# Attention of a gated cross-attention block: the value products of two steps issued together at the end of the odd step

## The chip, the cores and the metric

The kernel runs on one core of a Trainium2 chip. The metric is device time in microseconds (us) of one execution. The core has five instruction streams that run side by side and meet only at semaphores: PE (TensorE, matmuls, with its weight loads shown as PEld), DVE (VectorE), ACT (ScalarE), POOL (GpSimd) and SP (SyncE, which only issues DMAs here). Each stream is executed in the order in which it is written.

## The reference, cut to what matters

```python
# x (4,512,256), ctx (4,1024,256); 16 heads of 64; everything float32
lat = layer_norm(_layernorm(x), lat_g, lat_b);  ctx = layer_norm(ctx, ctx_g, ctx_b)
q = heads(lat @ Wq);  k, v = split(ctx @ Wkv);  k = rope(heads(k), cos, sin);  v = heads(v)
attn = softmax(clip(q @ k.T * 64**-0.5, -11, 11))
x = x + tanh(g_xattn) * (merge(attn @ v) @ Wo + bo)
# then a mixture of 4 experts, 2 per token (router, gelu MLP 256-1024-256), on layer_norm(x):
x = x + tanh(g_ffn) * moe(_layernorm(x))
```

## The kernel before

The attention is cut into 4 batches `b`, 4 units `u` of four heads, and 8 steps `s` per unit. A unit has two pairs of heads; steps 0 to 3 belong to the first pair and 4 to 7 to the second, and `c = s % 4` is the place within the pair. In the text a step is also given by `i = 8*u + s` (0 to 31 within a batch). A step takes 256 positions of the context, in two halves. For them it computes the scores of two heads against 512 queries (`score`, line 1909), exponentiates them (`exps`, ACT, line 989), clamps the result between the exponentials of -11 and 11 (`clamp`, DVE, line 1231, which writes `prob[:, s % 2]` in place), adds the probabilities to the running denominators (`sums`, DVE, line 1237; none at c = 0) and multiplies them with the values (`values`, PE, line 1924, 16 matmuls on 32-column strips of the array that accumulate in PSUM).

Beside that each step makes keys and values for the next unit: `kv_make` (PE, line 1890) multiplies, `kv_evac` (ACT, line 935) copies out, `rot_cos` (DVE, line 1218) and `rotate` (POOL, line 752, two operations, L757 and L761) apply the rotary embedding, and in the following step `k_turn` (PE, line 1901, L1906 in the profile) transposes the rotated keys into the bank `tr`. It first waits for `rot`, that is for POOL's second operation. `k_split` (ACT, line 929) and `k_low` (DVE, line 1183, L1186) then empty `tr`. All float32 products are made of three products of rounded parts (`three`, line 1861; lines 1863 to 1865).

The order on PE is written by hand in `step` (line 2044): the two score halves; `k_turn` of the previous step and `kv_make` (in steps i = 19 to 28 of a batch that has a successor, and in i = 9 and 10, `kv_make` comes first); at c = 0 `denominators` (L1946); at s = 2 and 3 the projection of the unit before (`project`); at c = 1 `q_make`; then `values` of the previous step; then, in steps i = 18 to 27 of batches 0 to 2, one transpose for the next batch's context or input into `tr` (`ctx_turn` L1870, `lat_turn` L1877), and in steps i = 8 and 9 one for the router (`x_turn` L1980). These transposes wait for `k_ready`, which `k_low` of the same step raises, since they write the bank that it reads. In the last unit of the last batch (`is_direct`) there are no keys to make and `direct` (L1961) sums the denominators on PE behind the values.

The scores of a step wait until the exponentials of the step before have read the same PSUM bank. `values` waits for the two clamps of its own step, and at c = 0 also for `normalise` (DVE, L1268) of the pair before, which reads the same output bank `pv`. The order on DVE within a step is: `q_low` (c = 2) or `normalise` (c = 1); clamp; clamp; `rot_cos`; `k_low`; `ctx_low` where the next batch is prepared; the two `sums`; `residual`; `reciprocals` (c = 0) or `o_low` (c = 1); statistics and normalisation of rows. POOL has, besides `rotate`, small scale computations for the next batch (`ctx_scale`, `lat_scale`, lines 717 to 742) and in the last batch the scatters of rows.

Of the kernel before, what the change touches and what calls it, by code (L numbers as in the profile page):

```python
# [33 lines left out]
def flamingo_kernel(nc, x, ctx_in, g_xattn, g_ffn, cos, sin, lat_g, lat_b, ctx_g, ctx_b, w_q, w_kv, w_o, b_o,  # L34
# [9 lines left out]
    UNITS = INNER // (4 * DH)  # L44
# [4 lines left out]
    STEPS = 2 * CH  # L49
# [15 lines left out]
    with ExitStack() as stack:  # L65
# [291 lines left out]
        def step_no(b, u, s):  # L357
            return b * BS + (u * STEPS + s)

        def tile_no(b, t):  # L360
            return b * ST + t

        def kv_no(b, u, t):
            return b * BS + (u * ST + t)

        def pair_no(b, p):
            return b * PAIRS + p
# [10 lines left out]
        def wait(eng, semaphore, count):  # L378

            if count > 0:  # L380
                eng.wait_ge(semaphore, count)
# [69 lines left out]
        def is_direct(b, u):  # L451

            return b == B - 1 and u == UNITS - 1

        def out_bank(b, p):

            return tr if b == B - 1 and p == PAIRS - 1 else pv
# [5 lines left out]
        def den_bank(b, p):  # L463

            return kv if b == B - 1 and p == PAIRS - 2 else mi
# [32 lines left out]
        def is_first(b, u):  # L498
            return b == 0 and u == 0
# [5 lines left out]
        def next_unit(b, u):  # L505
            return (b, u + 1) if u + 1 < UNITS else (b + 1, 0)

        def next_pair(b, p):
            return (b, p + 1) if p + 1 < PAIRS else (b + 1, 0)
# [1348 lines left out]
        def _(pe):  # L1858
# [31 lines left out]
            def kv_make(b, u, t):  # L1890
                pe.wait_ge(c_ready, tile_no(b, t) + 1)
                if b == 0 and t == 0:
                    pe.wait_ge(wkv_ready, u + 1)
                wait(pe, rot1, t - 1 if is_first(b, u) else kv_no(b, u, t))
                for k in range(KT):
                    last = three(kv_bank(b, u, t)[:].rearrange("p (w n) -> p w n", w=2), lambda l: ctx_t[:, l, k, t * P:(t + 1) * P],
                                 lambda l: wkv[:, l, k, :].rearrange("p (w n) -> p w n", w=2)[:, :, u * UW:(u + 1) * UW],
                                 k == 0, k == KT - 1)
                last.then_inc(kv_ready, 1)
# [9 lines left out]
            def score(b, u, s, i):  # L1909
                c, j, p = s % CH, s // CH, u * 2 + s // CH  # L1910
                t = 2 * c + i
                pe.wait_ge(k_ready, kv_no(b, u, t) + 1)
                if c == 0 and i == 0:
                    pe.wait_ge(q_ready, pair_no(b, p) + 1)

                wait(pe, exp_done[i], step_no(b, u, s))
                for lk, lq in ((0, 0), (0, 1), (1, 0)):
                    for h in range(2):
                        rows_h = slice(h * DH, (h + 1) * DH)
                        last = mm(sc[i][:, h * N:(h + 1) * N], kst[rows_h, u % 2, j, lk, t * P:(t + 1) * P],  # L1920
                                  q_sp[rows_h, p % 2, lq, :], start=lk + lq == 0, stop=lk == 1)
                last.then_inc(sc_ready[i], 1)

            def values(b, u, s):
                c, j, p = s % CH, s // CH, u * 2 + s // CH
                if c == 0 and out_bank(b, p) is tr:
                    pe.wait_ge(k_ready, B * BS)
                elif c == 0:

                    wait(pe, o_norm, pair_no(b, p))  # L1930
                for i in range(2):
                    pe.wait_ge(clamped[i], step_no(b, u, s) + 1)
                    for g in range(4):
                        half, h = g // 2, g % 2
                        at = (2 * j + h) * DH + half * 32
                        last = mm(out_bank(b, p)[g * 32:(g + 1) * 32, :], val[:, u % 2, 2 * c + i, at:at + 32],  # L1936
                                  prob[:, s % 2, i, h * N:(h + 1) * N], start=c == 0 and i == 0, stop=c == CH - 1 and i == 1)
                last.then_inc(pv_done, 1)
# [11 lines left out]
            def direct(b, u, s):  # L1950

                c, p = s % CH, u * 2 + s // CH
                if c == 0:
                    pe.wait_ge(den_turned, pair_no(b, p))
                    if p == PAIRS - 2:
                        pe.wait_ge(rot1, B * BS)
                for i in range(2):
                    for g in range(4):
                        half, h = g // 2, g % 2
                        at = h * N + half * QH  # L1960
                        last = mm(den_bank(b, p)[g * 32:(g + 1) * 32, 0:QH], ones[:, 0:32], prob[:, s % 2, i, at:at + QH],  # L1961
                                  start=c == 0 and i == 0, stop=c == CH - 1 and i == 1)
                if c == CH - 1:
                    last.then_inc(den_ready, 1)
# [79 lines left out]
            def step(b, u, s, last):  # L2044
                i = u * STEPS + s
                p, c = u * 2 + s // CH, s % CH
                make = not (last and u == UNITS - 1)
                nb, nu = next_unit(b, u)
                score(b, u, s, 0)
                score(b, u, s, 1)  # L2050
                asked = i - X_TURN in (1, 2)
                turned = asked or not last and 0 <= i - TURN - 1 < ST + 2
                if make and turned:
                    kv_make(nb, nu, s)
                if i == X_TURN + 3:
                    pe.wait_ge(f_lout, 2 * b + 3)
                if last and i == R_RANK + 3:
                    pe.wait_ge(r_read, 1)
                if s == 0 or make:

                    if asked:
                        router(b, i - X_TURN - 1, tr, 0, UW // E)
                    elif turned and i - TURN - 1 < ST:
                        pe.wait_ge(c_affd, tile_no(b + 1, i - TURN - 1) + 1)
                    elif turned:
                        pe.wait_ge(l_affd, 2 * (b + 1) + i - L_TURN)
                    k_turn(*((nb, nu, s - 1) if s else (b, u, ST - 1)))
                if make and not turned:
                    kv_make(nb, nu, s)
                if c == 0 and not (is_first(b, u) and s == 0):  # L2070

                    pe.wait_ge(q_ready, pair_no(b, p) + 1)
                    wait(pe, wo_out, (b * UNITS + u) * 2 - (2 if s == 0 else 0))
                    if not (is_direct(b, u) and s == CH):
                        denominators(*((b, p - 1) if p else (b - 1, PAIRS - 1)))
                if s in (2, 3) and not is_first(b, u):

                    pe.wait_ge(q_ready, pair_no(b, p + 1) + 1)
                    wait(pe, wo_out, (b * UNITS + u) * 2 + s - 4)
                    project(*((b, u - 1) if u else (b - 1, UNITS - 1)), s - 2)  # L2080
                if c == 1 and not (last and p == PAIRS - 1):

                    wait(pe, den_turned, pair_no(b, p))
                    q_make(*next_pair(b, p))
                if not (is_first(b, u) and s == 0):
                    values(*((b, u, s - 1) if s else (b, u - 1, STEPS - 1) if u else (b - 1, UNITS - 1, STEPS - 1)))
                if is_direct(b, u) and s:
                    direct(b, u, s - 1)
                if not last and TURN <= i < L_TURN + 2:

                    pe.wait_ge(k_ready, kv_no(nb, nu, s - 1) + 1 if s else kv_no(b, u, ST - 1) + 1)
                    if i < L_TURN:
                        ctx_turn(b + 1, i - TURN, tr)
                    else:
                        lat_turn(b + 1, i - L_TURN, tr)
                if i - X_TURN in (0, 1):

                    pe.wait_ge(k_ready, kv_no(nb, nu, s - 1) + 1 if s else kv_no(b, u, ST - 1) + 1)
                    pe.wait_ge(f_lout, 2 * b + i - X_TURN + 1)
                    pe.wait_ge(f_norm, b * NT + 2 * (i - X_TURN) + 2)  # L2100
                    x_turn(i - X_TURN, tr)
                if last and i == R_RANK + 1:
                    pe.wait_ge(k_ready, kv_no(nb, nu, s - 1) + 1)
                    count_slots()
                if is_direct(b, u) and s == SLOTS_AT:
                    pe.wait_ge(den_turned, B * PAIRS - 1)
                    slots_turn(0)
# [122 lines left out]
```

## Time and profile before

| | |
|---|---|
| median of 3 runs | 1106.79 us (1106.78 to 1106.92) |
| the profiled execution | 1109.79 us, span of its instructions 1108.1 us |
| mean granted clock of TensorE | 0.995 |
| busy over the span | PE 96%, DVE 85%, PEld 64%, ACT 59%, POOL 48% |
| the chain that ended last | PE 78%, DVE 14%, issue 3%, ACT 2% |
| attention steps | from 37 us to 849 us of the span |

A timeline row gives the start in us from the span's start, the time until its last instruction ends, the engine, the line, the operation, output and inputs with their shapes, and how many instructions are merged. In brackets stands the idle time of the engine before it and what ended it. A window row gives its bounds and length, the busy time (and number of instructions) of PE, PEld, DVE, ACT and POOL, the granted clock, the share of the DMA engines and their GB/s. The ends of matmuls are modelled, so the start of the next instruction tells more than the end of the last.

### The profile page before, as it was taken

Reading aid. Unit: us, or ns where it says so; the run is one execution under the profiler, and the core shown is the slowest. Engines: PE = TensorE matmul, PEld = TensorE weight load, DVE = VectorE, ACT = ScalarE, POOL = GpSimd, SP = SyncE. Lnnn points to the kernel's source line nnn. Section 1 sums busy time; section 2 is a strip of 40 time slices with the busy share of each in tenths; the row PEclk is TensorE's granted clock in tenths of the full one; section 3 lists DMA queues with packets and bytes.
Section 4 is the critical chain, followed back from the end, with each engine's and each line's share of the span. In section 5 each row is a group of like instructions: output and inputs, shape, how many; then the busy total and the mean of one; then the engine's idle time right before and its main releaser. Section 6 shows DMA issues by size and latency. Waiting matters only on the chain.

```text
span 1108.1 us, 22494 instructions
## 1 busy us (share of the span) xinstructions
PE 1069.2 (96%) x7965; PEld 712.2 (64%) x7965; DVE 946.6 (85%) x1765; ACT 655.8 (59%) x1269; POOL 532.3 (48%) x551
## 2 busy tenths in 40 slices
PE   5999999999999999999999999999999999999996
PEld 3556555655555555656555655665546998899995
DVE  7898999898989989898999898879988756876676
ACT  5655556664645765555566655544568565667663
POOL 7433375332437634342565353424761655655561
PEclk9999999999999999999999999999999999999998
DMA  7000010000000000001010000610165333555335
GB/s 200 25 10 11 20 39 11 20 11 11 10 20 23 27 11 11 13 8 30 1 44 15 11 11 10 192 54 20 50 213 181 106 116 130 178 194 189 116 115 181
DMA packets 60054, 73.10 MB, mean 66 GB/s; under 512 B 11420, under 2 KB 53032, under 8 KB 59945
## 3 DMA queue, kind: packets, MB, share of 16 engines
q1 hardware_dynamic: 56376, 62.87, 18.5%
q0 software_dynamic: 3264, 8.53, 2.0%
q8 instruction: 66, 1.08, 0.4%
q14 instruction: 44, 0.35, 0.1%
q10 hardware_dynamic: 304, 0.27, 0.1%
HBM read 54.84 MB, written 17.33 MB: 65 GB/s over the span
## 4 chain that ended last, share of the span: by engine, by line
PE 78%; DVE 14%; issue 3%; ACT 2%; DMA 1%; POOL 1%; another core or an unknown queue 0%; SPq 0%; DVEq 0%; POOLq 0%
PE pv L1936 16%; PE sc L1920 15%; PE kv L1863 6%; PE kv L1865 5%; PE kv L1864 5%; PE sc L1863 4%; PE sc L1865 4%; PE sc L1864 4%; PE tr L1906 3%; DVE acc L1249 3%; PE mi L1863 3%; PE mi L1864 2%; PE mi L1865 2%; PE mi L1946 2%; DVE prob L1234 2%
## 5 line engine op out<-in xcount | busy, mean ns | idle before, releaser
L997 ACT ACTIVATE prob<-sc 128x1024 f32<-128x1024 f32 x256 | 249.3, 1029 | 194.9 <-PE sc L1920 187.0
L757 POOL TENSOR_TENSOR rot_s<-k_raw,sinb 128x256 f32<-128x256 f32 x128 | 110.4, 862 | 380.7 <-ACT k_raw L940 380.6
L1936 PE MATMUL pv<-prob,val 128*32 128x512 f32 x1984 | 237.8, 597 | 1.1 <-DVE recip L1268 0.6
L1234 DVE TENSOR_SCALAR prob<-prob 128x1024 f32<-128x1024 f32 x256 | 183.2, 729 | 40.5 <-ACT prob L997 38.1
L1920 PE MATMUL sc<-q_hid,w2all 64*128 64x512 f32 x1536 | 213.3, 409 | 0.0
L1920 PEld LDWEIGHTS sc<-q_hid,w2all 64*128 64x128 f32 x1536 | 134.8, 185 | 100.2 <-issue 55.2
L1249 DVE TENSOR_TENSOR acc<-acc,prob 128x1024 f32<-128x1024 f32 x120 | 177.6, 1501 | 0.0
L761 POOL TENSOR_TENSOR rot_c<-rot_c,rot_s 128x256 f32<-128x256 f32 x128 | 109.6, 856 | 39.4 <-DVE rot_c L1222 24.9
L1936 PEld LDWEIGHTS pv<-prob,val 128*32 128x32 f32 x1984 | 54.8, 109 | 106.5 <-issue 86.9
L1863 PE MATMUL kv<-w2all,acts 128*128 128x512 f32 x248 | 109.9, 443 | 2.0 <-DVE acts L1180 2.0
L1865 PE MATMUL kv<-w2all,acts 128*128 128x512 f32 x248 | 98.6, 398 | 0.0
L1864 PE MATMUL kv<-w2all,acts 128*128 128x512 f32 x248 | 98.0, 395 | 0.0
L1863 PE MATMUL sc<-w2all,q_hid 128*128 x296 | 87.2, 295 | 7.3 <-DVE q_hid L1717 6.5
L1246 DVE TENSOR_TENSOR acc<-prob 128x1024 f32<-128x1024 f32 x60 | 84.8, 1452 | 0.0
L1864 PE MATMUL sc<-w2all,q_hid 128*128 x296 | 83.8, 283 | 0.0
L1865 PE MATMUL sc<-w2all,q_hid 128*128 x296 | 83.6, 282 | 0.0
L940 ACT ACTIVATE k_raw<-kv 128x256 f32<-128x256 f32 x124 | 48.6, 392 | 50.6 <-PE kv L1865 48.5
L1222 DVE TENSOR_TENSOR rot_c<-kv,cosb 128x256 f32<-128x256 f32 x124 | 52.1, 420 | 28.9 <-ACT val L941 23.0
L1717 DVE SCALAR_TENSOR_TENSOR q_hid<-sc,rot_c,q_hid 128x256 fp32r<-128x256 f32 x78 | 37.6, 482 | 36.5 <-ACT q_hid L1115 30.8
L1110 ACT ACTIVATE sc<-sc,c_aff 128x256 f32<-128x256 f32 x78 | 34.9, 448 | 54.2 <-PE sc L1865 50.2
L838 POOL TENSOR_TENSOR acts<-prob,acts 128x512 fp32r<-128x512 f32 x34 | 45.0, 1322 | 40.8 <-ACT acts L1030 39.6
L1863 PEld LDWEIGHTS sc<-w2all,q_hid 128*128 128x128 f32 x296 | 56.5, 191 | 10.4 <-issue 10.2
(346 smaller groups left out, 2409.9 us busy)
## 6 DMA issues: line engine op xcount, KB each, us to landing
prob<-in_L_ffn_w SPq DMA_DIRECT2D x17, 1024.0 KB, 5.2
slots_x<-lat_r SPq DMA_DIRECT2D x1, 5016.0 KB, 18.2
rows<-slots_x SPq DMA_DIRECT2D x19, 264.0 KB, 5.2
rows<-in_ctx SPq DMA_DIRECT2D x32, 128.0 KB, 2.2
w_raw<-in_L_xattn_Wq SPq DMA_DIRECT2D x16, 256.0 KB, 2.7
w_raw<-in_L_xattn_Wo SPq DMA_DIRECT2D x64, 64.0 KB
acc<-in_L_ffn_w SPq DMA_DIRECT2D x16, 256.0 KB, 4.1
acc<-in_L_ffn_w SPq DMA_DIRECT2D x5, 512.0 KB
```

What stands on the lines that cost most here:

```text
L757: g.tensor_tensor(rot_s[:].rearrange("p (h a c) -> p h a c", h=4, a=2), kh[:, :, ::-1, :], sinb[:, t].unsqueeze(1).to_broadcast([P, 4, 2, ...
L761: g.tensor_tensor(k_rot[:], rot_c[:], rot_s[:], ALU.add).then_inc(rot, 1)
L997: a.activation(prob[:, s % 2, i, :], sc[i][:], ACT.Exp, scale=DH ** -0.5).then_inc(exp_done[i], 1)
L1222: v.tensor_tensor(rot_c[:].rearrange("p (h c) -> p h c", h=8), kv_bank(b, u, t)[:, 0:UW].rearrange("p (h c) -> p h c", h=8), cosb[:, t].un ...
L1234: v.tensor_scalar(prob[:, s % 2, i, :], prob[:, s % 2, i, :], EXP_LOW, EXP_HIGH, ALU.max, ALU.min).then_inc(clamped[i], 1)
L1246: v.tensor_tensor(acc[:, i, :], prob[:, 0, i, :], prob[:, 1, i, :], ALU.add).then_inc(summed[i], 1)
L1249: v.tensor_tensor(acc[:, i, :], acc[:, i, :], prob[:, s % 2, i, :], ALU.add).then_inc(summed[i], 1)
L1863: mm(dst, lhs(0), rhs(0), start=start, stop=False, **kw)
L1864: mm(dst, lhs(0), rhs(1), start=False, stop=False, **kw)
L1865: return mm(dst, lhs(1), rhs(0), start=False, stop=stop, **kw)
L1920: last = mm(sc[i][:, h * N:(h + 1) * N], kst[rows_h, u % 2, j, lk, t * P:(t + 1) * P], q_sp[rows_h, p % 2, lq, :], start=lk + lq == 0, sto ...
L1936: last = mm(out_bank(b, p)[g * 32:(g + 1) * 32, :], val[:, u % 2, 2 * c + i, at:at + 32], prob[:, s % 2, i, h * N:(h + 1) * N], start=c == ...
```

## The change

In every unit but the last unit of the last batch, an even step issues no value products; an odd step issues those of the step before and its own, one behind the other, at the place where one such block stood. The last unit of the last batch keeps its order, but its first step has no block of the unit before any more, since the odd step 7 has issued it.

```diff
@@ PE, step(b, u, s, last)
                     wait(pe, den_turned, pair_no(b, p))
                     q_make(*next_pair(b, p))
-                if not (is_first(b, u) and s == 0):
-                    values(*((b, u, s - 1) if s else (b, u - 1, STEPS - 1) if u else (b - 1, UNITS - 1, STEPS - 1)))
                 if is_direct(b, u) and s:
+                    values(b, u, s - 1)
                     direct(b, u, s - 1)
+                elif s % 2 and not is_direct(b, u):
+                    values(b, u, s - 1)
+                    values(b, u, s)
                 if not last and TURN <= i < L_TURN + 2:
```

## Rows read from the trace of the kernel before

**Rows 1.** Busy time of each engine and granted clock (PEclk), attention steps.
```profile
37.00:849.00 812.00, 804.55 (x5888) 459.93 (x5892) 735.40 (x1250) 472.56 (x865) 365.74 (x377) 1.00 0.11 35
```
**Rows 2.** Timeline of PE, steps i = 14 and 15 of batch 2.
```profile
532.83 1.67 PE L1920 MATMUL sc<-q_hid,w2all 64*128 64x512 f32 x12
534.43 0.44 PE L1906 MATMUL tr<-ident,rot_c 128*128 128x128 f32 x2
...
535.87 0.40 PE L1865 MATMUL kv<-w2all,acts 128*128 128x512 f32 x1
536.20 1.92 PE L1936 MATMUL pv<-prob,val 128*32 128x512 f32 x16
538.05 1.65 PE L1920 MATMUL sc<-q_hid,w2all 64*128 64x512 f32 x12
...
543.26 1.66 PE L1920 MATMUL sc<-q_hid,w2all 64*128 64x512 f32 x12
```
**Rows 3.** Timelines of ACT, DVE and POOL, the same two steps.
```profile
533.85 1.94 ACT L997 ACTIVATE prob<-sc 128x1024 f32<-128x1024 f32 x2 [2.17 <-PE sc L1920]
...
537.40 0.41 DVE L1186 TENSOR_TENSOR w2all<-tr,w2all 128x256 fp32r<-128x256 f32 x1
537.74 2.85 DVE L1249 TENSOR_TENSOR acc<-acc,prob 128x1024 f32<-128x1024 f32 x2
...
540.51 1.28 DVE L1234 TENSOR_SCALAR prob<-prob 128x1024 f32<-128x1024 f32 x2
...
537.64 0.73 POOL L761 TENSOR_TENSOR rot_c<-rot_c,rot_s 128x256 f32<-128x256 f32 x1
```
**Rows 4.** Timeline of PE, step i = 28 of batch 3: values, direct, score.
```profile
830.57 1.92 PE L1936 MATMUL pv<-prob,val 128*32 128x512 f32 x16
832.31 1.05 PE L1961 MATMUL kv<-prob,ones 128*32 128x256 f32 x16
833.29 1.65 PE L1920 MATMUL sc<-q_hid,w2all 64*128 64x512 f32 x12
```
**Rows 5.** Timelines of PE and DVE, step i = 20 of batch 2.
```profile
574.12 1.07 PE L1946 MATMUL mi<-acc,ones 128*32 128x256 f32 x16
575.01 1.90 PE L1936 MATMUL pv<-prob,val 128*32 128x512 f32 x16
576.84 0.44 PE L1870 MATMUL tr<-ident,rows 128*128 128x128 f32 x2
577.21 0.97 PE L1920 MATMUL sc<-q_hid,w2all 64*128 64x512 f32 x6
...
575.27 0.41 DVE L1186 TENSOR_TENSOR w2all<-tr,w2all 128x256 fp32r<-128x256 f32 x1
```
**Rows 6.** Timelines of PE and DVE, step i = 22 of batch 2.
```profile
589.59 0.44 PE L1870 MATMUL tr<-ident,rows 128*128 128x128 f32 x2
...
589.12 0.41 DVE L1186 TENSOR_TENSOR w2all<-tr,w2all 128x256 fp32r<-128x256 f32 x1
```
**Rows 7.** Timelines of PE and DVE, step i = 8 of batch 2.
```profile
497.39 0.66 PE L1980 MATMUL tr<-ident,more 128*128 128x128 f32 x4
...
496.03 0.41 DVE L1186 TENSOR_TENSOR w2all<-tr,w2all 128x256 fp32r<-128x256 f32 x1
```
**Rows 8.** Timelines of POOL and PE, steps i = 16 and 17 of batch 2.
```profile
543.54 1.18 POOL L736 TENSOR_TENSOR l_rs<-l_mv,eps 128x4 f32<-128x4 f32 x1
...
550.34 0.73 POOL L761 TENSOR_TENSOR rot_c<-rot_c,rot_s 128x256 f32<-128x256 f32 x1
...
551.13 0.44 PE L1906 MATMUL tr<-ident,rot_c 128*128 128x128 f32 x2
```
**Rows 9.** Timeline of POOL, step i = 28 of batch 2 (begins at 624.17).
```profile
629.51 1.13 POOL L761 TENSOR_TENSOR rot_c<-rot_c,rot_s 128x256 f32<-128x256 f32 x1
```
**Rows 10.** Timelines of DVE and PE, batch 3, steps i = 15 and 25.
```profile
752.25 1.72 DVE L1234 TENSOR_SCALAR prob<-prob 128x1024 f32<-128x1024 f32 x2
...
814.39 1.92 PE L1936 MATMUL pv<-prob,val 128*32 128x512 f32 x16 [0.52 <-issue]
```

## The prediction

> **What bounds the kernel now.** I read the busy times over the attention steps first, then the timeline of PE through two plain steps, then the other engines in the same two steps. In the attention PE is busy 804.6 of 812.0 us at the full clock; DVE follows with 735.4, ACT has 472.6 and POOL 365.7 [rows 1]. The reader should see that PE hardly ever waits: each instruction of step 14 starts as the one before it drains [rows 2]. So a step costs what PE issues in it, and the other engines matter only where one of them makes PE wait. How near they are is in the third view. Keys made on PE in step 14 end at 535.87 + 0.40; ACT copies them, and POOL's second rotation ends at 537.64 + 0.73 = 538.37, which is 5.54 after the step's first score at 532.83 [rows 2, 3]. The transpose that needs them comes 1.60 into the next step, at 5.22 + 1.60 = 6.82. The slack of this chain is 1.3 us, and it exists because a block of values, 1.85 us, stands between the keys and the next step. That block is what the change takes out of even steps.
>
> **What a block costs and what joining saves.** From the first values matmul to the next score it is 538.05 - 536.20 = 1.85 [rows 2]; to a block that works on the same column strips it is 832.31 - 830.57 = 1.74 [rows 4]. I price the join of two value blocks at 1.74 + 1.85, so it saves 0.11. The entry is no saving: keys to values starts 0.33 after the last key matmul, and I take keys to score as the same, as both change the shape in the array. At c = 0 the denominators stand between: denominators to values takes 0.89 [rows 5], the same kind of block to a score 833.29 - 832.31 = 0.98 [rows 4], so 0.89 + 1.83 + 1.85 before and 0.98 + 1.74 + 1.85 after, which is 4.57 both times. So a pair of an even and an odd step gains 0.11 if c is 2 and 3, nothing if c is 0 and 1, where no wait is new. At best, if the shape change on both sides of a removed block (about 0.10 and 0.12) were all saved, it would be 0.22 in each of 60 pairs, 13 us; at worst joining saves nothing.
>
> The trace's 1.74 against 1.85 is a small gain from keeping the column strips. The Trainium skill (TensorE: Matmul & The Clock Gate, Part 3, The mechanism) says that weight loads overlap matmuls in flight only when the row group differs; all value matmuls use the whole height, so by it the join would drain like any other border and save nothing. The trace speaks against that, as 1.74 is less than 1.85.
>
> **Where PE will wait (the rotation).** Without the block step 14 is 536.20 - 532.83 = 3.37 long, and its successor wants the transposed keys at 3.37 + 1.60 = 4.97. POOL's add ends at 5.54 as before, since it hangs on ACT and on this step's keys, not on the values; PE resumes 0.06 behind it (550.34 + 0.73 = 551.07, then 551.13 [rows 8]). So PE waits 0.63 there. The pair takes 3.37 + 5.21 + 1.74 + 0.63 = 10.95 against 543.26 - 532.83 = 10.43: 0.52 more. This holds for pairs (6,7), (14,15) and (30,31) of a batch. The clamps of step 15 don't decide it, though closely: DVE's sums end at 540.59 and the two clamps at 541.79, 8.96 after the start [rows 3], and the second values block begins at 5.60 + 0.20 + 1.56 + 1.74 = 9.10. In pair (28,29) `kv_make` is first, the step would be 3.39 + 0.98 = 4.37, and POOL ends at 629.51 + 1.13 = 630.64, 6.47 after 624.17 [rows 9]: a wait of 6.53 - 5.96 = 0.57. In pair (16,17) POOL first has the scale chain of the next batch: from its start at 543.54 to the end of the add at 551.07 are 7.53 us [rows 8]. After the change it starts some 0.65 before step 16, when step 15's rotation is done, so the transpose goes at 6.94, not at 4.35 + 1.60: 1.00 of wait, of which 551.13 - 549.33 - 1.60 = 0.20 is there already (549.33 is the first score of step 17): 0.80 more. Pairs (0,1), (4,5) and (12,13) have the denominators, 4.35 + 1.60 = 5.95 against 5.60, and the project blocks of 1.4 us cover (2,3) and (10,11).
>
> **Where PE will wait (the bank `tr`).** The transposes for the next batch wait for `k_low`, which the values covered. In step 22 the values are no cover even now: `k_low` ends at 589.53 and the transpose starts at 589.59 [rows 6], 5.38 after the step's start at 584.21. Without the block PE is there at 3.40. `k_low` can't be done much before 4.84, since its chain goes through the exponentials, two copies and the clamps; in step 20 it ends at 575.27 + 0.41 = 575.68, 4.96 after 570.72 [rows 5]. With a transpose at 4.90 and 0.37 from it to the score [rows 5], steps 20, 22 and 24 become 5.27 to 5.30 long. They were 6.49, 5.75 and 6.48, and each gives 1.74 to its odd neighbour. Step 23 waits 0.6 for `k_low` today and no longer will. Per pair: (20,21) +0.55, (22,23) +0.64, (24,25) +0.55. Steps 18 and 26 have a project block and come out even (0 and -0.04). Step 8: `k_low` ends at 496.44, 5.12 after 491.32, the transpose at 497.39 leads to the score at 497.97 [rows 7]; with `k_low` at 4.98 the step is 5.62 instead of 6.65, and the pair gains 1.74 - 1.03 = 0.71 in length.
>
> **What queues behind the new waits.** Behind a waiting `k_turn` or transpose stand on PE the rest of the step and the next scores, behind which ACT's exponentials and then DVE's clamps stand. As odd steps grow by 1.74, DVE has caught up by the next even step, and no wait is passed on. No DMA, and no order on another queue, changes.
>
> **The sum.** Batches 1 and 2 each: 3 x 0.52 + 0.57 + 0.80 + 0.71 + 0.55 + 0.64 + 0.55 - 0.26 = 5.1. Batch 0: the same, 1.74 because the block of step 1 now stands in step 1, 0.63 for pair (2,3), which has no project block yet, and about 0.5 more at step 8: 8.0. Batch 3 prepares no batch but routes rows on DVE. 0.52 + 0.71 for pairs (6,7) and (8,9), -0.3 for those without a wait; in (14,15) the clamps of step 15 run at 752.25 to 753.97 [rows 10], 9.31 to 11.03 after step 14's start at 742.94, and the values of step 15 wait for them, +1.6, of which pair (16,17) gives 0.5 back; (20,21) waits 0.9 for POOL. That is 2.9, a sum of small walks, good to 3 us. The block that step 24 loses is no gain: values of step 24 stand at 814.39 after an idle time of PE [rows 10], held by DVE's chain to `normalise`, and whether PE gets there 1.85 earlier doesn't matter; this term lies between -1.85 and 0, and I take 0. The expert stage is not touched. Total 8.0 + 10.2 + 2.9 = 21.1 us. On the profiled execution, 1109.79 us (its span is 1108.1), that is 1130.9; it stands 3.00 above the median of the runs, so the forecast is 1106.79 + 21.1 = 1127.9, say 1128 us.
>
> **The rivals.** *The waits are larger.* The values of the odd step wait for its own clamps, for which the margin is 0.14 at the first half in pair (14,15). If DVE is 0.5 late in about half of the 60 pairs, 15 us come on top: 1143. For it speaks DVE's 91% in these steps [rows 1]; against it, that odd steps become longer and that the second half of a block has 0.85 more. If joining saves nothing, 0.11 x 60 = 6.6 come on top: 1134. Chance of over 1137: 0.14.
>
> *Faster, by the changes of shape.* If a removed border saves 0.22 in each of the 60 pairs, this is worth 13 us, and if copies and rotation are quicker when PE leaves them more time between bursts, so that the waits don't open, the time is 1094. It decides from the point where the key chain ends within 4.97 instead of 5.54. Against it: the chain's length is the same in nearly all plain steps, and every link of it is an engine's own duration. With the waits it is 1128 - 13 + 3 = 1118, still slower. Chance of a gain: 0.08.
>
> *No change.* The waits open, but what DVE and POOL were behind is made good in the longer odd steps, by about as much. Today's waits that could vanish are small: PE is idle 7.4 us of the attention in all [rows 1], against 21 of new ones. Near 1107, chance 0.05.
>
> **How the numbers follow.** The forecast's own case (1116 to 1137) has 0.73. A measurement of this kernel tells 0.2%, about 2.2 us, from no change. Faster 0.08, same 0.05, slower 0.87. The range takes the borders' ends (-10 and +6.6), and about a third of the waits either way: 1116 to 1138.
>
> **What would show it.** In the profile after: no values block in even steps, blocks of 32 matmuls some 3.55 us long in odd ones; idle time of PE or its weight loads before L1906 with POOL's L761 as releaser, 0.6 in steps 7, 15 and 31 of a batch and about 1.0 in step 17; idle time before L1870 and L1980 with DVE's L1186 as releaser, 1.4 in step 22; pair (14,15) 10.95 long, pair (4,5) unchanged at about 12.6. The forecast is wrong if POOL's add ends earlier after the score than 5.54, if the join costs or saves more than 0.11, or if the values of odd steps wait for the clamps (L1234) outside the last batch.

## The result and the profile after

The changed kernel takes 1133.22 us (median of 4 runs, 1132.55 to 1136.86) against 1106.86 (1106.78 to 1107.45) for the kernel before in the same session: a ratio of 1.025, 95% interval 1.0238 to 1.0262. It is slower by 26.4 us; 21 were forecast, as 1128 in 1116 to 1138. Its profiled execution took 1132.68 us, with a span of 1130.9.

First the busy times over the attention, which now ends at 875 and not at 849. The row has the same columns as [rows 1] and answers to it.

```profile
37.00:875.00 838.00, 801.61 (x5886) 463.09 (x5890) 739.86 (x1250) 472.05 (x864) 366.96 (x378) 1.00 0.11 34
```

PE was without work for 812.0 - 804.6 = 7.4 us and is now for 838.0 - 801.6 = 36.4. Its busy time even fell by 2.9. So the matmuls are not dearer: PE waits 29 us more. What it waits for is in the view of waits (engine and line that wait, engine and line that end it: us in total, times, longest), of the kernel after:

```profile
PEld tr L1906 <- POOL rot_c L761: 31.9, 37, 2.7
PE tr L1906 <- POOL rot_c L761: 17.2, 24, 2.5
PEld tr L1870 <- DVE w2all L1186: 16.0, 12, 2.2
PE tr L1870 <- DVE w2all L1186: 11.8, 12, 1.9
PEld pv L1936 <- DVE prob L1234: 11.4, 22, 2.3
```

The same rows of the kernel before:

```profile
PEld tr L1906 <- POOL rot_c L761: 13.6, 19, 2.4
PE tr L1906 <- POOL rot_c L761: 5.7, 6, 2.2
PEld tr L1870 <- DVE w2all L1186: 7.2, 6, 1.4
PE tr L1870 <- DVE w2all L1186: 1.6, 3, 0.5
PEld pv L1936 <- DVE prob L1234: 9.0, 28, 0.4
```

PE's own idle time before the key transposes grew by 11.5 us and before the next batch's transposes by 10.2, which is 21.7 of the 29. The rest is spread over the router's transposes (L1980), the input's (L1877) and, in batch 3, the values. Steps 14 to 17 of batch 2 on PE and POOL, which answer to [rows 2, 8], show how one such wait looks:

```profile
551.99 1.65 PE L1920 MATMUL sc<-q_hid,w2all 64*128 64x512 f32 x12
...
555.33 1.65 PE L1920 MATMUL sc<-q_hid,w2all 64*128 64x512 f32 x12
...
557.56 0.44 PE L1906 MATMUL tr<-ident,rot_c 128*128 128x128 f32 x2 [0.58 <-POOL rot_c L761]
...
559.33 3.64 PE L1936 MATMUL pv<-prob,val 128*32 128x512 f32 x32
562.90 1.67 PE L1920 MATMUL sc<-q_hid,w2all 64*128 64x512 f32 x12
...
570.17 0.44 PE L1906 MATMUL tr<-ident,rot_c 128*128 128x128 f32 x2 [1.26 <-POOL rot_c L761]
...
556.78 0.72 POOL L761 TENSOR_TENSOR rot_c<-rot_c,rot_s 128x256 f32<-128x256 f32 x1
...
561.89 0.73 POOL L761 TENSOR_TENSOR rot_c<-rot_c,rot_s 128x256 f32<-128x256 f32 x1 [0.96 <-DVE rot_c L1222]
562.58 1.18 POOL L736 TENSOR_TENSOR l_rs<-l_mv,eps 128x4 f32<-128x4 f32 x1
...
569.39 0.73 POOL L761 TENSOR_TENSOR rot_c<-rot_c,rot_s 128x256 f32<-128x256 f32 x1
```

Step 14 is 555.33 - 551.99 = 3.34 long, without a block of values. POOL's add ends at 557.50, 5.51 after the step's first score (5.54 was expected), and the transpose goes 0.06 later. The joined values take 562.90 - 559.33 = 3.57, where two single blocks took 3.70.

From the first scores of even steps comes the length of each pair of steps. This table is worked out from the timelines of PE; it has the change against the kernel before, in us, for batch 2 (for the kernels of the experiments too, which are told below):

```
pair      before  forecast  after     e1      e2     e3     e4     f2     f3     f4     g1
(0,1)     12.64      0      -0.01   +0.06   +0.01  +0.06   0.00  -0.02  +0.08  -0.01  +1.71
(2,3)     13.27    -0.11    -0.14   -0.10   -0.16  -0.11  -0.14  -0.14  -0.10   0.00  -0.14
(4,5)     12.64      0       0.00   +0.08    0.00  +0.08   0.00  +0.01  +0.08  +0.01  -1.71
(6,7)     10.43    +0.52    +0.49   -0.11   -1.22  -1.82  +0.48  +0.48  -1.82  -0.01  +0.40
(8,9)     14.72    +0.71    +0.69   +0.70   +2.31  +2.93  +0.69  +0.70  +1.72  +0.01  +2.32
(10,11)   14.15    -0.11    -0.13   -0.08   -0.12  -0.08  -0.13  -0.12  -0.08  -0.01  -0.12
(12,13)   12.64      0      +0.01   +0.08    0.00  +0.08  +0.01   0.00  +0.08  +0.01  -1.71
(14,15)   10.43    +0.52    +0.48   +0.40   +0.48  +0.40  +0.48  +0.48  -0.11  -0.01  -0.02
(16,17)   12.85    +0.80    +1.12   -0.13   -0.59  -1.83  +1.11  -0.21  -1.89  -0.21  +0.85
(18,19)   14.61      0      -0.46   +0.65*  +0.58  +1.43  -0.46  -0.46  +0.95  -0.30  -0.01
(20,21)   13.49    +0.55    +1.45   +1.40*   0.00   0.00  +1.47  +0.51   0.00   0.00   0.00
(22,23)   11.95    +0.64    +1.13   +2.64*  +0.02  +0.01  +0.65  +1.14  -0.57  -0.58   0.00
(24,25)   13.48    +0.55    +0.52   +0.51   +0.01  +0.01  +0.50  +0.51  +0.02  +0.01  +0.01
(26,27)   14.53    -0.04    +0.43   +0.42   +1.71  +1.71  -0.06  +0.44  +1.70   0.00   0.00
(28,29)   12.69    +0.57    +0.54   +0.07   +0.51  +0.07  +0.51  +0.54  +0.07  -0.01  -0.01
(30,31)   10.42    +0.52    +0.78   +0.72   +0.77  +0.72  +0.78  +0.50  -0.10   0.00   0.00
sum                 5.1      6.9     7.3     4.3    3.7    5.9    4.4    0.0   -1.1   +1.6
* batch 0 has -0.14, +0.52 and +1.13; why batch 2 differs is told with the first experiment
```

Where a kernel issues a block one pair earlier or later, two entries shift by 1.7 in opposite directions; there only sums over neighbours count. Batches 0, 1 and 3 of the kernel after have 9.6, 8.4 and 1.0, with 0.26 ahead of step 0; its attention ends 26.15 us later. The span grew by 22.8 only, because the profiled execution of before had a pause of 3.42 us in the expert stage that the profile after lacks, and stood 3.0 above its median (the columns of the row below are those of [rows 3]). Otherwise the expert stage is the same.

```profile
938.28 0.45 ACT L1110 ACTIVATE sc<-sc,c_aff 128x256 f32<-128x256 f32 x1 [3.42 <-remote]
```

### The profile page after: what moved, and what is told of

Same layout as the page of the kernel before. It is cut to its first block, busy times and chain, and to the rows that moved or that the text cites. A ratio compares the mean times of both kernels' runs of the same rounds, so it can differ in the third digit from the quotient of the medians.

```text
span 1130.9 us, 22494 instructions
## 1 busy us (share of the span) xinstructions
PE 1066.8 (94%) x7965; PEld 716.1 (63%) x7965; DVE 950.6 (84%) x1765; ACT 655.6 (58%) x1269; POOL 532.7 (47%) x551
## 4 chain that ended last, share of the span: by engine, by line
PE 70%; DVE 14%; issue 5%; ACT 4%; POOL 4%; DMA 1%; SPq 0%; DVEq 0%; POOLq 0%
PE pv L1936 16%; PE sc L1920 11%; PE kv L1863 5%; PE sc L1863 4%; PE kv L1865 4%; PE kv L1864 4%; PE sc L1864 4%; PE sc L1865 4%; DVE acc L1249 4%; PE tr L1906 3%; PE mi L1863 2%; PE mi L1865 2%; PE mi L1864 2%; ACT prob L997 2%; DVE prob L1234 2%
## 5 line engine op out<-in xcount | busy, mean ns | idle before, releaser
L757 POOL TENSOR_TENSOR rot_s<-k_raw,sinb 128x256 f32<-128x256 f32 x128 | 114.0, 890 | 386.5 <-ACT k_raw L940 386.4
L1234 DVE TENSOR_SCALAR prob<-prob 128x1024 f32<-128x1024 f32 x256 | 194.5, 773 | 55.2 <-ACT prob L997 53.5
L1936 PE MATMUL pv<-prob,val 128*32 128x512 f32 x1984 | 226.9, 595 | 4.1 <-DVE recip L1268 2.5
L1249 DVE TENSOR_TENSOR acc<-acc,prob 128x1024 f32<-128x1024 f32 x120 | 175.2, 1481 | 0.0
L1936 PEld LDWEIGHTS pv<-prob,val 128*32 128x32 f32 x1984 | 57.5, 109 | 134.4 <-issue 117.2
L1906 PE MATMUL tr<-ident,rot_c 128*128 128x128 f32 x256 | 54.2, 294 | 17.3 <-POOL rot_c L761 17.2
L1906 PEld LDWEIGHTS tr<-ident,rot_c 128*128 128x128 f32 x256 | 29.2, 144 | 54.1 <-POOL rot_c L761 31.9
```

Of the source, the lines that this page charges most:

```text
L757: g.tensor_tensor(rot_s[:].rearrange("p (h a c) -> p h a c", h=4, a=2), kh[:, :, ::-1, :], sinb[:, t].unsqueeze(1).to_broadcast([P, 4, 2, ...
L1234: v.tensor_scalar(prob[:, s % 2, i, :], prob[:, s % 2, i, :], EXP_LOW, EXP_HIGH, ALU.max, ALU.min).then_inc(clamped[i], 1)
L1249: v.tensor_tensor(acc[:, i, :], acc[:, i, :], prob[:, s % 2, i, :], ALU.add).then_inc(summed[i], 1)
L1906: last = nc.tensor.transpose(tr[:, j * P:(j + 1) * P], k_rot[:, j * P:(j + 1) * P], ident[:])
```

## The experiments

My theory after the first look was the prediction's: without its block, an even step comes to a transpose before the keys or the bank are ready. Two places were larger than forecast, (20,21) and (22,23), and there I blamed the order on DVE and ACT. The rival was that DVE, at 91% busy, is a second limit right beneath, so that no mended order on PE would win the waits back. The first four experiments ran on a chip on which the kernel before had 1110.31 us, the others on chips where it had 1106.07, 1109.68 and 1105.85. So times are compared by their ratios to the kernel before on the same chip; the kernel after has 1.025.

### Keys made first in every odd step

```diff
                 turned = asked or not last and 0 <= i - TURN - 1 < ST + 2
-                if make and turned:
+                early = turned or s % 2
+                if make and early:
                     kv_make(nb, nu, s)
...
-                if make and not turned:
+                if make and not early:
                     kv_make(nb, nu, s)
```

> The changed kernel, but in every odd step kv_make stands ahead of k_turn. Theory (PE waits because the block that covered the chain of keys is gone): the 0.6 us waits for POOL's add in steps 3, 7, 15 and 31, the 0.55 in 29 and the 1.2 in 17 go, 12.5 us in all, 1133.2 to about 1121. Rival (the odd step's values wait for DVE's clamps, and DVE sets the pace): nothing to gain, 1131 to 1134.

Measured: 1130.23 us, ratio 1.0172 (1.0133 to 1.0211). Some 8 us of the loss are gone by the ratios (6 by the pairs of the profiles), where 12.5 were expected: 1121 would have been a ratio of 1.013. The waits for POOL went as expected; steps 14 and 15 on PE, and DVE's clamps:

```profile
551.13 0.50 PE L1863 MATMUL kv<-w2all,acts 128*128 128x512 f32 x1
...
552.62 0.38 PE L1906 MATMUL tr<-ident,rot_c 128*128 128x128 f32 x2
552.93 1.92 PE L1936 MATMUL pv<-prob,val 128*32 128x512 f32 x16
555.16 1.92 PE L1936 MATMUL pv<-prob,val 128*32 128x512 f32 x16 [0.30 <-DVE prob L1234]
...
553.87 1.83 DVE L1234 TENSOR_SCALAR prob<-prob 128x1024 f32<-128x1024 f32 x2
```

The transpose stands behind the keys and waits for nothing, and 0.5 us later the values of step 15 wait for their own clamps. Pair (14,15) goes from +0.48 to +0.40, not to -0.11: one wait taken away uncovers another of nearly the same size. In (16,17), (28,29) and, in batches 1 to 3, (6,7) nothing takes the wait's place, and in (20,21) of batches 0 and 1 DVE's lag is gone (+0.52). The uncovered wait speaks for the rival.

Batch 2 shows how little slack DVE has. In step 18 it waited for rows of the next batch that a DMA brought:

```profile
571.75 0.43 DVE L1160 BATCH_NORM_STATS2 c_bn<-rows 128x6 f32<-128x256 f32 x1 [0.21 <-DMA rows<-in_ctx]
```

Against batch 1, where all ran alike until then, this instruction starts 0.28 later, `k_low` of the same step 0.77 later and that of the next step 1.18 later. PE waits for it in steps 18 and 20, and the pairs (18,19) and (20,21) cost 0.8 and 0.9 more than in batch 1, at the full clock. The excess of (22,23) is another thing, a stretch of TensorE at 1.2 GHz (last section).

### Single blocks kept ahead of the transposes

Odd steps 7 (all batches) and 17, 19, 21, 23, 25 (batches 0 to 2) issue only the block of the step before. The edit is shown against the kernel before; the call of `values` there is gone.

```diff
+            issued = [-1]
+            def joins(b, i):
+                return not (i == 7 or b < B - 1 and i in (17, 19, 21, 23, 25))
...
+                upto = step_no(b, u, s) - 1
+                if s % 2 and not is_direct(b, u) and joins(b, i):
+                    upto += 1
+                while issued[0] < upto:
+                    issued[0] += 1
+                    nb_, ni_ = divmod(issued[0], BS)
+                    values(nb_, ni_ // STEPS, ni_ % STEPS)
```

> The changed kernel, but the odd steps 7 (all batches) and 17, 19, 21, 23, 25 (batches that have a successor) issue only the values of the step before, so that the even steps with a transpose into tr behind them keep their block. Theory: pairs (8,9) and (18,19) to (26,27) return to their old lengths, -2.9 and -3.1 x 3, and the clock drop seen behind the 1.9 us wait in batch 1 goes: 1133.2 to about 1121. Rival (DVE sets the pace): less than 4 us back.

Measured: 1129.29 us, 1.017 (1.0139 to 1.0201), where 1.013 was expected. Steps 20 to 25 are as before the change, all 3.1 us of them won back in batch 2, so those waits are the missing blocks' doing. The stretch at 1.2 GHz in batch 1 is gone too, as expected. But (6,7) and (8,9) together are +1.09 after +1.18, although step 8 has its block again. Step 8 is 7.25 us long, not 6.65: its key transpose now waits 0.53 for POOL, behind the 0.59 in step 7.

### Both

> Both edits in one: keys first in odd steps, and blocks kept ahead of the transposes. Theory: the two kinds of wait are separate, so the gains add: 1133.2 - 12.5 - 12.3 = 1108.4, within 3 us of the kernel before. Rival (one underlying limit, DVE's load): the sum is clearly less than the parts, 1115 or more.

Measured: 1124.91 us, 1.0125 (1.0098 to 1.0151). It was expected within 3 us of before, and it is 14 above: the case of 1115 or more. The two edits don't add up. PE's waits for POOL at the key transposes fell from 17.2 to 7.4 us, and pairs (6,7) and (8,9) still cost -1.82 + 2.93 = 1.11. That is one wait for POOL in step 8:

```profile
501.97 0.44 PE L1906 MATMUL tr<-ident,rot_c 128*128 128x128 f32 x2 [1.14 <-POOL rot_c L761]
...
500.28 1.63 POOL L761 TENSOR_TENSOR rot_c<-rot_c,rot_s 128x256 f32<-128x256 f32 x1
```

POOL has the router's statistics ahead of this rotation (two operations, 1.19 and 2.24 us), and the add itself takes 1.63, where 0.73 is its usual time. So moving `kv_make` forward on PE can't help there.

### ACT's queries first

ACT rounds the next queries before it scales the next batch's rows, so that the exponentials behind them start earlier in steps 22 and 26.

```diff
+                if c == 1 and not (last and p == PAIRS - 1):
+                    q_round(*next_pair(b, p))
                 if not last and 0 <= i - TURN < ST:
...
-                if c == 1 and not (last and p == PAIRS - 1):
-                    q_round(*next_pair(b, p))
```

> The changed kernel, but on ACT q_round stands ahead of ctx_affine and lat_affine at c = 1. Theory (steps 22 and 26 gave nothing back because the exponentials stand behind the copy of the queries on ACT, at 1.97 instead of 1.49 after the score): these steps shrink by 0.48 each, 1133.2 to about 1130.3. Rival (k_low is late there because DVE lags): no change, 1133.

Measured: 1133.08 us, 1.0194 (1.0167 to 1.0221). The pairs moved just as expected, (22,23) from 1.13 to 0.65 and (26,27) from +0.43 to -0.06. These six moves are worth 2.9 us. The times are no measure of that: by the ratios the kernel is 6 us below the kernel after, and the profiled execution stood 2.6 above its median, with 3.06 more in (12,13) of batch 3 than the kernel after, where TensorE ran at 1.2 GHz for a stretch. So the cause at these two steps is shown by the pairs and not by the time.

### The kernel after once more, and each with light sums

To see what DVE does beneath, `sums` at c = 2 and 3 got 64 of 1024 columns, in the kernel after, in the kernel of both edits and in the kernel before. The denominators are incomplete; all waits stay.

```diff
-                    v.tensor_tensor(acc[:, i, :], acc[:, i, :], prob[:, s % 2, i, :], ALU.add).then_inc(summed[i], 1)
+                    v.tensor_tensor(acc[:, i, 0:64], acc[:, i, 0:64], prob[:, s % 2, i, 0:64], ALU.add).then_inc(summed[i], 1)
```

> The changed kernel itself, beside the three below on the same chip, since the chip of the first four edits ran the kernel before at 1110.3 instead of 1106.9. Both theories: 1.025 of the kernel before.

> The changed kernel with DVE's running sums at c = 2 and 3 over 64 of 1024 columns, so that the denominators are left incomplete; DVE has 2.7 us less to do in each of these steps. Theory A (DVE's load is the limit beneath the waits): waits that hang on DVE go, (20,21) falls from +1.46 to +0.55, (30,31) from +0.78 to +0.5, (14,15) of batch 3 from +2.1 to +0.5, about 6 us less than the changed kernel; the waits for POOL's add in steps 7, 15, 31 (+0.5 a pair) and for k_low in steps 20 to 24 stay. Theory B (chains of single waits, DVE's load of no account): the same time as the changed kernel within 1 us.

> The kernel with both edits (keys first in odd steps, blocks kept ahead of the transposes), with the same light sums. Theory A: with DVE out of the way the two edits take away all but a few waits, within 0.3% of the kernel before, 15 us less than the same kernel with full sums. Theory B: as with full sums, 1.2 to 1.3% above the kernel before.

> Control: the kernel before with the same light sums. Both theories: TensorE sets the pace there, so lighter sums are worth little, 0 to 3 us less (what DVE holds up in steps 12 to 24 of batch 3).

Measured on one chip, with the kernel before at 1106.07: after again 1133.64 (1.0246, 1.0229 to 1.0263); after with light sums 1120.63 (1.0129, 1.0113 to 1.0146), 13.0 less where 6 were expected; both edits with light sums 1101.62 (0.9955, 0.9941 to 0.9969), 0.45% below before, where within 0.3% was expected; before with light sums 1096.52 (0.9914, 0.9897 to 0.993), 9.5 less where 0 to 3 were expected. The last is the miss that taught most: the kernel before looks bound by PE alone, and pays for DVE too, 1.1 us in each of batches 0 to 2 and 6.3 in batch 3 by the profiles (of these 2.15 in (12,13), where the profile of before has a stretch at 1.2 GHz and this one has none).

Busy times over the attention, of both edits with light sums and then of before with light sums (columns as in [rows 1]):

```profile
35.00:848.00 813.00, 806.96 (x5907) 466.62 (x5908) 616.49 (x1254) 475.69 (x870) 309.40 (x379) 1.00 0.11 35
```

```profile
37.00:840.00 803.00, 801.85 (x5891) 459.51 (x5894) 613.07 (x1250) 472.81 (x865) 308.75 (x378) 1.00 0.11 35
```

With both the order mended and DVE light, PE is idle 6.0 us, as little as before the change. The plain pairs tell the two limits apart (us against before):

```
                    after   e1 keys  e3 both  f2 DVE   f3 both and
                            first    orders   light    DVE light
(14,15)             +0.48   +0.40    +0.40    +0.48    -0.11
(6,7) and (8,9)     +1.18   +0.59    +1.11    +1.18    -0.10
(30,31)             +0.78   +0.72    +0.72    +0.50    -0.10
```

Neither a better order alone nor a lighter DVE alone brings these pairs back; only both together do, and then the join's saving of 0.1 shows. In (14,15) and (30,31) the second chain, right behind the one through ACT and POOL to the keys, is DVE's own clamps: with keys made first PE waits 0.30 and 0.61 for them (L1234). In (6,7) and (8,9) it is POOL's: the add that took 1.63 above takes 0.75 with both edits and light sums, the statistic ahead of it 1.48 and not 2.24, and PE doesn't wait in step 8. Light sums thus lighten two engines, and this pair doesn't tell them apart. At (16,17) and (20,21) either is enough: light sums alone take +1.12 to -0.21 and +1.45 to +0.51, and so do keys made first, to -0.13 and (batches 0 and 1) +0.52. With light sums the joined kernel is still 5.1 us above the single one; in the profiled executions it is 7.1 (1103.68 and 1096.57), of which 3.9 stand in (12,13) of batch 3 (+1.70 and -2.15), where the joined one had a stretch at 1.2 GHz and the single one none.

### Joins only where they were free

Blocks are joined only in odd steps 1 and 3 (batches 1 to 3), 9 and 11, whose pairs had cost nothing or saved 0.13. All else is as before; the edit is the one of the second experiment with another `joins`:

```diff
             def joins(b, i):
-                return not (i == 7 or b < B - 1 and i in (17, 19, 21, 23, 25))
+                return i in (9, 11) or b and i in (1, 3)
```

> Value blocks joined only in steps 1 and 3 (not in batch 0) and 9 and 11, where the even steps 2, 4, 10 and 12 have a project block or the denominators as cover; all else as in the kernel before. Theory (where there is cover, the join saves 0.11 to 0.14 if the next score needs no new wait): -0.14 x 3 and -0.13 x 4 for (2,3) and (10,11), and in batch 3 the wait ahead of step 13 shortens by 1.4: 0.1 to 0.2% faster than the kernel before. Rival (each joined block lets DVE fall behind in the next pair): the same or slower.

Measured: 1116.22 us, 1.0049 (1.003 to 1.0067): slower by half a per cent, as the rival said. The joined pairs save their 0.12 to 0.14. But (6,7) costs 0.40, (8,9) 2.32 - 1.71 = 0.61 and (16,17) 0.85. These are waits for POOL's rotation in steps 7 and 8, four and five steps behind the join in 3, and in step 17, six behind the join in 11. In batch 2, POOL's add in step 7 and the key transpose of step 17:

```profile
489.86 0.73 POOL L761 TENSOR_TENSOR rot_c<-rot_c,rot_s 128x256 f32<-128x256 f32 x1 [1.77 <-DVE rot_c L1222]
...
555.38 0.44 PE L1906 MATMUL tr<-ident,rot_c 128*128 128x128 f32 x2 [0.97 <-POOL rot_c L761]
```

A join shortens the even step behind it by 1.7 us, and DVE has the same work there. Its first clamp in step 5 starts 3.73 after the score, where it started 2.15 before; in step 7 it is 4.08 against 3.04. POOL's rotation waits for DVE, and only where the order on PE leaves no slack PE waits for POOL. Behind the join in 11 the lag runs through two pairs that lose nothing. The 1.4 us expected in batch 3, ahead of step 13, didn't come. What the kernel after has there, -1.45, is a stretch at 1.2 GHz that its profile lacks and that those of before and of this kernel have (last section).

### POOL takes a part of DVE's sums

As light sums made the kernel before faster, one way to lighten DVE that keeps the whole computation was tried there: POOL adds the second half's probabilities in steps 14 and 15 of batch 3, and ACT rounds queries first (the edit of the fourth experiment). DVE leaves these two sums out; POOL's part of the edit:

```diff
+                if to_pool(b, u, s):
+                    pool.wait_ge(clamped[1], step_no(b, u, s) + 1)
+                    pool.wait_ge(summed[1], pair_no(b, u * 2 + s // CH) * 3 + s % CH - 1)
+                    g.tensor_tensor(acc[:, 1, :], acc[:, 1, :], prob[:, s % 2, 1, :], ALU.add).then_inc(summed[1], 1)
```

> The kernel before (old order of the value blocks) with two edits that relieve what the light sums pointed at: POOL makes the second running sum of steps 14 and 15 of batch 3, and on ACT q_round stands ahead of ctx_affine and lat_affine at c = 1. If DVE's lag in batch 3 costs the kernel before what the light sums showed in pair (16,17) (-1.46), this gives back about 1.5 us there, and 0.15 us in each step 22: about 2 us or 0.2% faster. Rival: POOL's sum, longer than DVE's 1.5 us, holds up the rotation or the scatters behind it, and the time stays or rises.

Measured: 1106.1 us, 0.9999 (0.999 to 1.0009). There is no gain. One such sum on POOL, from this kernel's timeline:

```profile
746.73 3.37 POOL L892 TENSOR_TENSOR acc<-acc,prob 128x1024 f32<-128x1024 f32 x1
```

It takes 3.37 us, where DVE does two in 2.85 [rows 3]. The pairs show two effects that cancel. ACT's new order gives 0.72 in (22,23) of each of batches 0 to 2, 2.2 in all, where 0.15 each was expected. POOL's sums cost 2.11 in (16,17) of batch 3. All other pairs stand within 0.05 of before. Beside the sum on POOL, a small operation of DVE (24 columns, for the router) took 2.10 us, which takes 0.18 in the kernel before. So DVE gained nothing by the sum that it was spared: its clamps of step 15 start 1.3 later, POOL's rotation waits for DVE, and in step 16 PE waits for the rotation and then, at the denominators, for POOL's second sum (in this kernel L1914 is the key transpose, L1954 the denominators, L765 the rotation's add and L892 the sum):

```profile
748.04 2.10 DVE L1551 TENSOR_TENSOR lat_r<-lat_r,spans 128x24 f32<-128x24 f32 x1
...
754.40 0.44 PE L1914 MATMUL tr<-ident,rot_c 128*128 128x128 f32 x2 [1.09 <-POOL rot_c L765]
...
757.72 0.64 PE L1954 MATMUL mi<-acc,ones 128*32 128x256 f32 x8 [0.92 <-POOL acc L892]
```

No version with the whole computation beat the kernel before. The one that these pairs point at, ACT's order alone in the kernel before, was not run.

## Why the prediction was right, and where it was short

**The direction and the cause are right.** The block of values was the cover of two chains, and the waits stand where they were looked for. Right within 0.05 us are pairs (6,7), (14,15) and (28,29) with their wait for POOL (0.49, 0.48, 0.54 for 0.52, 0.52, 0.57), pairs (8,9) and (24,25) (0.69 and 0.52 for 0.71 and 0.55), the pairs with denominators at 0, and the saving of a join (0.12 to 0.14 for 0.11, so the shape change on both sides of a removed block isn't saved a second time). Key chain and transpose came 5.51 and 5.57 after the score, for 5.54 and 5.60. Taken to the letter, all three of the prediction's signs of being wrong came: the add ends 0.03 earlier, the join saves 0.01 to 0.03 more, and values of an odd step wait for their clamps outside the last batch too, in step 31 of batches 0 to 2. The first two are of no weight; the third is part of what follows.

**The step that failed** (the direction and the range held, so it is a step within a right forecast) is "As odd steps grow by 1.74, DVE has caught up by the next even step, and no wait is passed on". It hasn't. In step 20 of batch 2, which answers to [rows 5], the clamps run from 594.34 and `k_low` ends at 596.41 + 0.41 = 596.82, 5.80 after the score, where 4.84 was expected:

```profile
591.02 1.66 PE L1920 MATMUL sc<-q_hid,w2all 64*128 64x512 f32 x12
...
596.88 0.44 PE L1870 MATMUL tr<-ident,rows 128*128 128x128 f32 x2 [1.39 <-DVE w2all L1186]
...
592.24 1.21 DVE L1249 TENSOR_TENSOR acc<-acc,prob 128x1024 f32<-128x1024 f32 x1
...
594.34 0.68 DVE L1234 TENSOR_SCALAR prob<-prob 128x1024 f32<-128x1024 f32 x1
...
596.41 0.41 DVE L1186 TENSOR_TENSOR w2all<-tr,w2all 128x256 fp32r<-128x256 f32 x1
```

With light sums the same transpose goes 4.91 after the score, as the forecast had it (4.90). The row stands between the scores of steps 20 and 21:

```profile
584.18 1.66 PE L1920 MATMUL sc<-q_hid,w2all 64*128 64x512 f32 x12
589.09 0.44 PE L1870 MATMUL tr<-ident,rows 128*128 128x128 f32 x2 [0.44 <-DVE w2all L1186]
589.45 1.65 PE L1920 MATMUL sc<-q_hid,w2all 64*128 64x512 f32 x12
```

The step is 589.45 - 584.18 = 5.27 long. This passed-on lag is worth 0.9 us in (20,21), 0.3 in (16,17), where POOL's scale chain starts late behind a rotation that waits 0.96 for DVE, and 0.3 in (30,31), where the second block of step 31 waits for its clamps. The block's first weights come 6.0 after the step's score at 664.58, and 5.7 with light sums:

```profile
670.57 0.16 PEld L1936 LDWEIGHTS pv<-prob,val 128*32 128x32 f32 x8 [0.99 <-DVE prob L1234]
```

Light sums remove the lag in all three, in (16,17) with the whole wait.

**Steps 22 and 26** were expected with `k_low` at 4.84 like the others. That floor was taken without ACT's place in the row: at c = 2 the exponentials stand behind `q_round`. Step 22 of batch 2 on PE and ACT answers to [rows 6]:

```profile
605.96 1.66 PE L1920 MATMUL sc<-q_hid,w2all 64*128 64x512 f32 x12
...
611.35 0.44 PE L1870 MATMUL tr<-ident,rows 128*128 128x128 f32 x2 [1.93 <-DVE w2all L1186]
...
607.45 0.61 ACT L987 ACTIVATE q_hid<-mi 128x512 fp32r<-128x512 f32 x1
607.93 1.96 ACT L997 ACTIVATE prob<-sc 128x1024 f32<-128x1024 f32 x2
```

The exponentials start 1.97 after the score, and the transpose goes at 5.39, to the hundredth as before the change (5.38). So the step keeps its length and its odd neighbour gets the block: +0.5 in (22,23) and in (26,27). The rounding put first removes just that.

**The sum.** Forecast and measured: batch 0 8.0 and 9.6; batch 1 5.1 and 8.4, of which 1.5 are a stretch at 1.2 GHz; batch 2 5.1 and 6.9; batch 3 2.9 and 1.0. In batch 2 the lag of DVE is 0.9 + 0.3 + 0.3 = 1.5, ACT's order 1.0, and (18,19) gives 0.5 back, 0.3 of it a wait for DVE in step 18 that the kernel before had; the rest is within 0.05 per pair. Batch 3 was a sum of small walks and only by luck near: 1.45 of what it lacks is a stretch at 1.2 GHz that the profile of before has in (12,13) (last section), the values of step 15 do wait for their clamps (+2.09 for +1.6), and more than forecast is given back later, -0.90 in (18,19) and -1.68 in (24,25). With light sums (14,15) is +0.49.

```profile
778.22 1.92 PE L1936 MATMUL pv<-prob,val 128*32 128x512 f32 x16 [1.37 <-DVE prob L1234]
```

**The rivals.** *The waits are larger* was right in its mechanism and given too little: DVE is late behind short steps, mostly in places other than its own clamps, and at about 5 us, not 15. *Faster, by the changes of shape* and *no change* are refuted: a joined block saves no more than 0.14, and the longer odd steps don't pay back.

## What to carry to other kernels

A block that an engine does "in any case" may be what covers the chains behind it; before it is moved, compare for each waiting instruction the time at which the engine would come with the time at which the releaser ends, in every step form, not in an average one. Where a second engine is at 90%, a step that gets shorter doesn't only open its own wait: the lag is carried on, here up to six steps, to wherever the order leaves no slack. An idle time of PE near zero doesn't show that the other engines are free; making one of them lighter in a trial does.

## What the hardware showed that was not expected

**DVE and POOL slow each other.** From batch 2 of the kernel after, a POOL operation, and beside it a clamp of the same shape as the one of 0.68 us above:

```profile
570.87 1.31 POOL L750 TENSOR_TENSOR wo<-w_raw,wo 128x512 fp32r<-128x512 f32 x1
...
570.99 1.74 DVE L1234 TENSOR_SCALAR prob<-prob 128x1024 f32<-128x1024 f32 x1
```

The clamp took 1.74 us, and ended 0.55 after POOL did. And POOL's own busy time over the attention of the kernel before fell from 365.74 to 308.75 us when only DVE's sums were shortened, with 377 and 378 instructions: so DVE's sums had cost POOL 57 us, which is why light sums also moved waits for POOL. The other way round, the sum of 3.37 us on POOL held a DVE operation of 0.18 us for 2.10 (last experiment). The Trainium skill (SBUF — State Buffer, Who interferes with whom) says that DVE and GpSimd share a port pair, and that whichever issues first has it for its whole instruction while the other is blocked. The trace agrees about, if the clamp is taken to need 0.68 from the end of POOL's operation: 570.87 + 1.31 + 0.68 = 572.86 against an end at 572.73.

**TensorE's clock fell behind some waits, not behind others.** In batch 1 the transpose of step 22 came after 1.92 us of waiting, and less than 3 us behind it matmuls of 0.39 us took 0.63. The columns of the last two rows are those of [rows 1]:

```profile
398.01 0.44 PE L1870 MATMUL tr<-ident,rows 128*128 128x128 f32 x2 [1.92 <-DVE w2all L1186]
...
400.76 0.63 PE L1864 MATMUL kv<-w2all,acts 128*128 128x512 f32 x1
```

```profile
392.00:398.00 6.00, 4.09 (x26) 2.58 (x22) 4.19 (x10) 4.64 (x10) 2.85 (x4) 1.00 0.09 22
398.00:402.00 4.00, 3.99 (x18) 2.78 (x19) 4.00 (x6) 3.33 (x6) 3.42 (x3) 0.71 0.00 0
```

The granted clock was 0.71 over these 4 us, which is a stretch at 1.2 GHz and the rest at 2.4. That pair cost 2.67 where the same pair of batch 2, behind a wait of 1.93, cost 1.13: 1.5 us. The kernel before had one such stretch, in (12,13) of batch 3, which the profile after lacks; its absence accounts for the -1.45 there, which is no gain of the change. The second profile of the kernel after shows it: with a stretch there it has +0.06. The window of before:

```profile
735.00:743.00 8.00, 8.00 (x44) 4.71 (x43) 3.82 (x7) 4.03 (x7) 1.47 (x2) 0.79 0.00 1
```

Of twelve profiles the four with a wait of 1.9 us in step 22 of batches 0 to 2 show a fall behind it in 5 of 12 places, and the eight without this wait in none; in (12,13) of batch 3 stretches come and go in both kernels. So the new wait of 1.9 us cost more than its length in some executions: a part of the sum that no pair's working had. Which wait is followed by a fall was not settled.
